# Top-64 attention on one core: threshold counts by ScalarE sums, or by signs summed on TensorE

## The chip, the core and the metric

The kernel runs on one core of a Trainium2 chip. The metric is the device time in microseconds of one execution; smaller is better. The engines are TensorE (PE in the profile, its weight loads PEld), VectorE (DVE), ScalarE (ACT), GpSimd (POOL) and SyncE (SP), which issues the DMAs. Each works through its own list of instructions in order and waits on semaphores for the others.

## What is computed

The reference is one gated cross-attention block with top-k selection and a small quantised feed-forward step, for 32 batches of 256 tokens and width 256:

```python
Q = (layernorm(x) @ Wq.T + bq).reshape(b, 16, 256, 16)      # 16 heads of 256 rows
K, V = ...                                                  # the same from the context
scores = einsum('bhqd,bhkd->bhqk', Q, K) / 4
topk_scores, topk_idx = top_k(scores, 64)                   # 64 of the 256 keys of each row
attn = softmax(topk_scores) @ V[topk_idx]
x = x + tanh(g_xattn) * (attn.reshape(b, 256, 256) @ Wo.T + bo)
x = x + tanh(g_ffn) * fp8_gemm(layernorm(x), kernel) ...    # 256 x 256, then bias
```

The costly part is the selection: 32 batches of 16 heads of 256 rows, each needing its 64 largest of 256 scores. The scores are needed to full precision, so queries and keys are split into three bf16 levels, and a product over 96 rows gives them.

## The kernel before

**Halves and tiles.** A batch has two halves (`g`) of 8 heads; half `i = 2b + g`. A head is two tiles of 128 rows by 256 keys, so a half has 16 tiles (`GT`). `scores` makes the score tiles on PE in `ps_s`, and `copy_scores` on DVE copies them to `score_sb`, with each row's maximum in `mx`. Four halves are held (`RING`).

**Guide rounds.** No row is sorted. A threshold X is looked for of each row, above which some 57 to 64 of its scores lie. It begins at a quarter of the row's maximum (`start_thresholds`). In each of four rounds (`GUIDES`) the scores above it are counted (`guide_counts`): ACT does 15 of the 16 tiles (`ACT_TILES`, L880), each with one Sign of X minus score summed along the row by the accumulator; DVE does the last (L1068). `update_thresholds` (L1072 on) on DVE then steps X, by a slope in round 0 and by a chord between the nearest points on both sides later; a step is a chain of small operations on 128x16, each waiting for the one before it. The next count waits for it (`s_thr`), and it waits for the count (`s_cnt`, `s_dcnt`).

**Final tiles and thresholds.** Once the four rounds of half i are done, and while those of half i + 1 run, `final_tiles` on DVE takes four tiles a round: compare with X and count (L1146), push the scores above X down by a huge number (L1151, four tiles at once), and take the next eight below it (MAX8, L1157). `final_thresholds` picks from these eight, by the count, the 64th score (`thr`) and the 65th. A row where these can't be told apart or found is unsure. PE sums the unsure rows of each tile (`sum_unsure`), DVE reads the sum (`read_unsure`, `convert_unsure`, `settle`) and, where it is not zero, searches the tile in eight rounds of maxima and replacements (`select_tile`, L1192, L1194).

**Masks, exponents, mix.** `masks_of` on ACT (L891) writes `unfit`, Relu of `thr` minus score, which is above zero for a score not selected; it waits for `settle`. `exponents` on PE makes the head's scores again, by key, less the row's maximum, in `ps_e`, and adds the mask times -2^100 (L712, L716). ACT takes the exponential (L900), and `mix` multiplies by the values in f32 (L731). These lag the masks by 2 and 4 heads (`MASK_LAG`, `MIX_LAG`).

**The rest of a batch.** Front: layernorm, transposes, projections q, k, v in f32 (L664 to L686), two or three batches ahead; GpSimd splits q and k in levels, and DMAs lay them out by head. Back: output projection (L742), residual, second layernorm, quantised feed-forward, two or three batches behind. The order of the work is written out by hand in each engine's `batch` function. PSUM's eight banks are `ps_s` (two), `ps_e` (two), `ps_o`, `ps_a`, `ps_b` and `ps_x`.

## Time and profile before

| | |
|---|---|
| median of 3 runs | 3271.35 us (3269.1 to 3274.13) |
| profiled execution | 3268.81 us |
| its span, first to last instruction | 3266.9 us |
| mean granted TensorE clock | 0.717 of full speed |
| busy: PE, DVE, ACT, POOL | 54%, 82%, 84%, 30% |
| DMA | mean 51 GB/s |

A busy share is the time in which the engine had an instruction recorded. Instructions of one engine overlap somewhat in the records, so the cost of one in a row of like ones is read from start to start, not from its duration. A granted clock of 1 is 2.4 GHz, 0.5 is 1.2 GHz; a value between is a mix of the two over the stretch.

### The profile page before, as it was taken

How to read it: one execution, taken by the hardware profiler on the slowest of the kernel's cores; microseconds unless marked ns; L12 is line 12 of the kernel's file. 1: busy time of each engine (PE TensorE's matmuls, PEld its weight loads, DVE VectorE, ACT ScalarE, POOL GpSimd, SP SyncE). 2: the span in 40 equal slices, each digit the busy share in tenths (PEclk: the TensorE clock that was granted, in tenths of full speed). 3: DMA queues.
4: the chain of work that ended last, by engine and by line, in shares of the span. 5: the costliest groups of instructions: out<-in, count | busy, mean ns of one | idle time of the engine just before them, and what ended most of it. 6: DMA issues, size and time to landing. Idle time of an engine off the chain costs nothing.

```text
span 3266.9 us, 51511 instructions
## 1 busy us (share of the span) xinstructions
PE 1780.4 (54%) x7952; PEld 950.5 (29%) x7952; DVE 2691.6 (82%) x11883; ACT 2730.3 (84%) x9638; POOL 966.1 (30%) x1174
## 2 busy tenths in 40 slices
PE   3245555555465555455556556564556556454555
PEld 2122233332233233232323333332233223232222
DVE  1678888888888888888888888888888888888884
ACT  1888888998788898797889998988798788997983
POOL 5122223233222233232233223333223233232112
PEclk8567677777677777776667777767676767777777
DMA  4223332223333223331233333223333133331211
GB/s 70 38 43 60 49 47 52 52 49 63 52 52 54 45 49 63 52 55 34 48 64 56 60 48 56 48 48 64 53 49 55 33 62 61 55 54 33 40 24 46
DMA packets 451902, 166.43 MB, mean 51 GB/s; under 512 B 245616, under 2 KB 451440, under 8 KB 451520
## 3 DMA queue, kind: packets, MB, share of 16 engines
q1 hardware_dynamic: 451136, 162.38, 28.4%
q14 instruction: 310, 2.54, 0.3%
q8 instruction: 72, 1.18, 0.2%
q0 software_dynamic: 384, 0.33, 0.1%
HBM read 102.57 MB, written 59.24 MB: 50 GB/s over the span
## 4 chain that ended last, share of the span: by engine, by line
DVE 36%; ACT 30%; issue 17%; PE 14%; DVEq 2%; POOL 1%; ACTq 0%; DMA 0%; SPq 0%; POOLq 0%; another core or an unknown queue 0%
ACT act_junk L880 22%; DVE masked L1151 5%; DVE score_sb L1047 4%; PE ps_o L731 4%; DVE following L1157 4%; DVE masked L1146 3%; ACT unfit L891 3%; ACT pT_sb L900 2%; PE ps_a L684 2%; DVE X L1083 2%; PE ps_b L675 2%; PE ps_e L712 1%; PE ps_a L686 1%; DVE chord L1115 1%; PE ps_e L716 1%
## 5 line engine op out<-in xcount | busy, mean ns | idle before, releaser
L880 ACT ACTIVATE act_junk<-score_sb,X 128x256 int8<-128x256 f32 x3840 | 1892.1, 503 | 211.3 <-DVE X L1121 183.2
L712 PE MATMUL ps_e<-qs,ks 99*128 99x256 bf16 x1024 | 348.2, 350 | 1321.7 <-ACT pT_sb L900 1321.7
L731 PE MATMUL ps_o<-pT_sb,v_aug 128*32 128x256 f32 x2048 | 766.4, 514 | 0.5 <-ACT pT_sb L900 0.5
L880 ACT ACTIVATION_READ_ACCUMULATOR act_junk<-score_sb,X 128x1 f32 x3840 | 755.0, 197 | 0.0
L891 ACT ACTIVATE unfit<-score_sb,thr 128x256 bf16<-128x256 f32 x1024 | 463.1, 504 | 218.0 <-DVEq L1241 214.6
L1047 DVE TENSOR_SCALAR_CACHE_REDUCE score_sb<-ps_s 128x256 f32<-128x256 f32 x1024 | 418.8, 415 | 142.1 <-PE ps_s L698 140.0
L712 PEld LDWEIGHTS ps_e<-qs,ks 99*128 99x128 bf16 x1024 | 121.9, 119 | 1403.6 <-ACT unfit L891 1199.5
L1146 DVE TENSOR_SCALAR_CACHE_REDUCE masked<-score_sb,X 128x256 f32<-128x256 f32 x1024 | 426.3, 472 | 19.1 <-DVE x_res L1294 8.4
L1157 DVE MAX8 following<-masked 128x8 f32<-128x256 f32 x1024 | 357.7, 409 | 1.7 <-issue 0.7
L540 POOL CAST split<-proj 128x512 bf16<-128x512 f32 x64 | 48.0, 750 | 1042.8 <-ACT proj L866 1027.2
L716 PE MATMUL ps_e<-dropb,unfit 128*128 128x128 bf16 x2048 | 355.9, 273 | 0.0
L1151 DVE SCALAR_TENSOR_TENSOR masked<-masked,score_sb 128x1024 f32<-128x1024 f32 x256 | 336.8, 1316 | 0.4
L900 ACT ACTIVATE pT_sb<-ps_e 128x512 f32<-128x512 f32 x512 | 301.7, 590 | 11.9 <-PE ps_o L731 11.8
L731 PEld LDWEIGHTS ps_o<-pT_sb,v_aug 128*32 128x32 f32 x2048 | 231.9, 136 | 266.4 <-issue 191.0
L716 PEld LDWEIGHTS ps_e<-dropb,unfit 128*128 128x128 bf16 x2048 | 253.3, 124 | 52.4
L698 PE MATMUL ps_s<-ks,qs 96*128 96x256 bf16 x1024 | 228.2, 311 | 67.7 <-DVE score_sb L1047 35.1
L1083 DVE TENSOR_TENSOR X<-aim,count 128x16 f32<-128x16 f32 x256 | 82.3, 322 | 200.8 <-ACT act_junk L880 167.3
L510 POOL TENSOR_SCALAR var<-mv 128x2 f32<-128x2 f32 x64 | 14.6, 228 | 579.4 <-DVE mv L994 576.5
L1068 DVE SCALAR_TENSOR_TENSOR dve_junk<-score_sb,X,minus_twos 128x256 bf16<-128x256 f32 x256 | 158.2, 618 | 0.1
L698 PEld LDWEIGHTS ps_s<-ks,qs 96*128 96x128 bf16 x1024 | 74.8, 102 | 269.8 <-issue 206.2
L602 POOL TENSOR_TENSOR rest<-y_sb,magic_sb 128x512 f32<-128x512 f32 x32 | 43.9, 1371 | 362.4 <-DVE magic_sb L1020 362.4
L559 POOL COPY qs<-rows 96x4096 bf16<-96x4096 bf16 x32 | 127.2, 3974 | 22.7 <-DMA rows<-q_scr 11.6
(158 smaller groups left out, 3332.8 us busy)
## 6 DMA issues: line engine op xcount, KB each, us to landing
rows<-q_scr SPq DMA_DIRECT2D x192, 128.0 KB, 5.1
rows<-k_scr SPq DMA_DIRECT2D x192, 128.0 KB, 5.0
o_scr<-o_sb SPq DMA_DIRECT2D x128, 128.0 KB, 2.7
q_scr<-split SPq DMA_DIRECT2D x32, 384.0 KB, 2.7
k_scr<-split SPq DMA_DIRECT2D x32, 384.0 KB, 2.7
x_in<-in_x SPq DMA_DIRECT2D x32, 256.0 KB, 3.1
ctx_sb<-in_ctx SPq DMA_DIRECT2D x32, 256.0 KB, 2.7
v_scr<-proj SPq DMA_DIRECT2D x32, 256.0 KB, 5.8
```

What stands on the lines that cost most here:

```text
L698: ins = nc.tensor.matmul(ps_s[:, n % 2, jh * TOK:(jh + 1) * TOK], qs[u][0:SPLITS, h, 8 * jh:8 * jh + 8, :].rearrange("d j t -> d (j t)"), ...
L712: nc.tensor.matmul(ps_e[:, n % 2, kc * TOK:(kc + 1) * TOK], ks[u][:, h, 8 * kc:8 * kc + 8, :].rearrange("d j t -> d (j t)"), qs[u][:, h, : ...
L716: ins = nc.tensor.matmul(ps_e[:, n % 2, kc * TOK + jh * P:kc * TOK + jh * P + P], unfit[:, n % MASKS, jh, kc * P:kc * P + P], dropb[:], st ...
L731: ins = nc.tensor.matmul(ps_o[32 * c:32 * c + 32, half * TOK:(half + 1) * TOK], v_aug[p][:, 2 * h + kc, :], pT_sb[:, n % 2, kc * TOK:(kc + ...
L880: ins = nc.scalar.activation(act_junk[:, t, :], score_sb[:, slot, t, :], ACT.Sign, scale=-1.0, bias=X[slot % 2][:, 0, t:t + 1], accum_out= ...
L891: ins = nc.scalar.activation(unfit[:, n % MASKS, jh, :], score_sb[:, slot, t, :], ACT.Relu, scale=-1.0, bias=thr[:, slot, t:t + 1])
L900: nc.scalar.activation(pT_sb[:, n % 2, :], ps_e[:, n % 2, :], ACT.Exp).then_inc(s_PT, 1)
L1047: ins = nc.vector.tensor_scalar(score_sb[:, slot, t, :], ps_s[:, n % 2, jh * TOK:(jh + 1) * TOK], 0.0, None, ALU.add, ALU.max, accum_out=m ...
L1068: ins = nc.vector.scalar_tensor_tensor(dve_junk[:, t - ACT_TILES, :], score_sb[:, slot, t, :], X[slot % 2][:, 0, t:t + 1], minus_twos[:].t ...
L1146: nc.vector.tensor_scalar(masked[:, k, :], score_sb[:, slot, t, :], X[slot % 2][:, 0, t:t + 1], None, ALU.is_gt, ALU.add, accum_out=final_ ...
L1151: nc.vector.scalar_tensor_tensor(masked[:], masked[:], -BIG, scores, ALU.mult, ALU.add).then_inc(s_fin, 1)
L1157: nc.vector.max(following[:, t, 1:], masked[:, k, :]).then_inc(s_fin, 1)
```

## The change

All counts of a guide round go over TensorE. For each of the half's 8 heads PE makes the scores again, this time with the keys on the partitions (`scores_by_key`), in one of three banks `ps_t`. Two more matmuls subtract each row's threshold (`less_thresholds`), from X transposed on PE (`transpose_thresholds`) and negated by ACT into bf16 (`negate_thresholds`). ACT takes one Sign of the head's 128x512 differences from PSUM, with no bias and no accumulator, into bf16 (`signs`). PE sums the signs over the keys with four matmuls by a column of ones (`tally`), and DVE reads the counts from PSUM. So that the subtraction is exact, X is kept as a value that bf16 can hold: each step is written to bf16 first (`started`, `stepped`).

DVE no longer counts a guide tile. The count at the final X, before made by DVE's compare, is now made on ACT, four tiles a round (`final_counts`). DVE's compare and push-down of four tiles becomes one operation a tile, the score times (score not above X). `final_thresholds` has two more small operations. The masks move from ACT to DVE: one compare a tile of the score with `thr`, written as bf16 1 or 0. The exponents share the three banks, and both lags become one of 2 heads. The projections, the output and the feed-forward step share one bank `ps_a`, and the transposed thresholds and counts one, `ps_c`. PE's, ACT's, DVE's and SP's orders are written anew around this.

```diff
@@ PE @@
+            def transpose_thresholds(i, slot, r):
+                pe.wait_ge(s_thr, GUIDES * i + r + 1)
+                pe.wait_ge(s_crd, GUIDES * i + r)
+                nc.tensor.transpose(ps_xt, X[slot][:, 0, :], ident[:]).then_inc(s_xt, 1)
+            def scores_by_key(u, g, n, bank):
+                h = head_of(g, n)
+                for kc in range(2):
+                    nc.tensor.matmul(ps_t[:, bank, kc * TOK:(kc + 1) * TOK],
+                                     ks[u][0:SPLITS, h, 8 * kc:8 * kc + 8, :].rearrange("d j t -> d (j t)"),
+                                     qs[u][0:SPLITS, h, :, :].rearrange("d j t -> d (j t)"), start=(kc == 0), stop=False,
+                                     skip_group_check=True)
+            def less_thresholds(i, r, n, bank):
+                if n == 0:
+                    pe.wait_ge(s_mx, GUIDES * i + r + 1)
+                both_chunks = minus_x[:].rearrange("t (o q) -> t o q", o=1).to_broadcast([GT, 2, P])
+                for jh in range(2):
+                    ins = nc.tensor.matmul(ps_t[:, bank, :].rearrange("p (c j q) -> p c j q", c=2, j=2)[:, :, jh, :],
+                                           identb[0:GT, 2 * n + jh:2 * n + jh + 1].to_broadcast([GT, P]), both_chunks,
+                                           start=False, stop=(jh == 1), skip_group_check=True)
+                ins.then_inc(s_R, 1)
+            def tally(i, par, r, n, buf):
+                pe.wait_ge(s_G, GUIDES * GH * i + GH * r + n + 1)
+                for jh in range(2):
+                    for kc in range(2):
+                        ins = nc.tensor.matmul(ps_cnt[par][:, 2 * n + jh:2 * n + jh + 1],
+                                               sign[:, buf, kc * TOK + jh * P:kc * TOK + jh * P + P], ones_b[:],
+                                               start=(kc == 0), stop=(kc == 1))
+                if n == GH - 1:
+                    ins.then_inc(s_cnt, 1)
+            def count_round(b, p, u, g, r, phase, first, second, last, middle):
...
+                scores_by_key(u, g, 0, bank[0])
+                scores_by_key(u, g, 1, bank[1])
+                less_thresholds(i, r, 0, bank[0])
+                less_thresholds(i, r, 1, bank[1])
+                if last:
+                    exponent_taken(*last)
+                for n in (2, 3):
+                    scores_by_key(u, g, n, bank[n])
+                    less_thresholds(i, r, n, bank[n])
+                    tally(i, slot % 2, r, n - 2, buf[n - 2])
+                if first:
+                    exponents(*first, bank[4], False)
+                if middle:
+                    middle()
+                for n in (4, 5):
+                    tally(i, slot % 2, r, n - 2, buf[n - 2])
+                    scores_by_key(u, g, n, bank[n + 1])
+                    less_thresholds(i, r, n, bank[n + 1])
+                if first:
+                    exponent_taken(*first)
+                for n in (6, 7):
+                    scores_by_key(u, g, n, bank[n + 1])
+                    less_thresholds(i, r, n, bank[n + 1])
+                    tally(i, slot % 2, r, n - 2, buf[n - 2])
+                if second:
+                    exponents(*second, bank[9], False)
+                for n in (6, 7):
+                    tally(i, slot % 2, r, n, buf[n])
@@ PE, batch, each round r @@
+                        if guided:
+                            count_round(cb, cp, cu, cg, r, phase, first, second, last, middle)
...
+                        if has(2) and (g, r) == (0, 0):
+                            transpose_tokens(b + 2)
...
+                        if first:
+                            mix(*first)
+                        if second:
+                            mix(*second)
+                        for k in (2 * r + 2, 2 * r + 3):
+                            if k < GH and has(1):
+                                scores(b + 1, (u + 1) % OPS, g, k, 2 * b + g - 1 if k == 2 and mixes else None)
...
+                        if r < GUIDES - 1 and guided:
+                            transpose_thresholds(2 * cb + cg, 2 * cp + cg, r + 1)
@@ ACT @@
-            def guide_counts(i, slot, r):
...
-            def masks_of(i, slot, n):
...
+            def negate_thresholds(i, r):
+                act.wait_ge(s_xt, GUIDES * i + r + 1)
+                nc.scalar.activation(minus_x[:], ps_xt, ACT.Copy, scale=-1.0).then_inc(s_mx, 1)
+            def signs(i, r, n, buf, bank):
+                act.wait_ge(s_R, GUIDES * GH * i + GH * r + n + 1)
+                nc.scalar.activation(sign[:, buf, :], ps_t[:, bank, :], ACT.Sign).then_inc(s_G, 1)
+            def final_counts(i, slot, t):
...
+                ins = nc.scalar.activation(act_junk[:, t % JUNK, :], score_sb[:, slot, t, :], ACT.Sign, scale=-1.0,
+                                           bias=X[slot][:, 0, t:t + 1], accum_out=final_count[:, t:t + 1])
+            def round_of_signs(i, r, phase, i_final, final_slot, first, second, mixed):
...
+                    negate_thresholds(i, r)
+                for n in range(GH):
+                    if i is not None:
+                        signs(i, r, n, sign_buffer(phase, r, n), bank[n if n < 4 else n + 1])
+                    if n == 3 and first:
+                        exps(*first, bank[4])
+                    if n == 3 and mixed:
+                        evacuate_mixed(*mixed)
+                    if n == 7 and second:
+                        exps(*second, bank[9])
+                    if n % 2 and i_final is not None:
+                        final_counts(i_final, final_slot, 4 * r + n // 2)
@@ DVE @@
-            def guide_counts(i, slot, r):
...
-                nc.vector.tensor_tensor(x[:, 1, :], aim[:], count[slot % 2][:], ALU.subtract).then_inc(s_upd, 1)
+                nc.vector.tensor_scalar(x[:, 1, :], ps_cnt[slot % 2], TOK - 2 * AIM, None, ALU.add).then_inc(s_crd, 1)
...
-                nc.vector.tensor_tensor(newton[:], newton[:], x[:, 0, :], ALU.add)
+                nc.vector.tensor_tensor(stepped[:, 0, :], newton[:], x[:, 0, :], ALU.add)
...
-                    nc.vector.tensor_scalar(masked[:, k, :], score_sb[:, slot, t, :], X[slot % 2][:, 0, t:t + 1], None,
-                                            ALU.is_gt, ALU.add, accum_out=final_count[:, t:t + 1]).then_inc(s_fin, 1)
+                    nc.vector.scalar_tensor_tensor(masked[:, k, :], score_sb[:, slot, t, :], X[slot][:, 0, t:t + 1],
+                                                   score_sb[:, slot, t, :], ALU.is_le, ALU.mult).then_inc(s_fin, 1)
...
-                nc.vector.scalar_tensor_tensor(masked[:], masked[:], -BIG, scores,
-                                               ALU.mult, ALU.add).then_inc(s_fin, 1)
...
+            def masks_of(i, slot, n):
+                H = GH * i + n
+                dve.wait_ge(s_T, at(H - MASKS + 1))
+                carry(dve)
+                for jh in range(2):
+                    t = 2 * n + jh
+                    ins = nc.vector.tensor_scalar(unfit[:, n % MASKS, jh, :], score_sb[:, slot, t, :], thr[:, slot, t:t + 1], None,
+                                                  ALU.is_lt)
+                ins.then_inc(s_P, 1)
@@ SP, batch @@
+                if has(1):
+                    store_values(b + 1)
                 if has(3):
                     load_front(b + 3)
...
+                if has(-1):
+                    move_out(b - 1)
                 if has(1):
                     move_values(b + 1, 1 - p)
-                if has(-1):
-                    move_out(b - 1)
```

On DVE a round r of half i is now: four products of the final tiles, two copies of scores, the read of the unsure rows (round 0), four maxima, two copies, `settle` (round 0), four masks, `start_thresholds` (round 3), the update of half i + 1's thresholds, in round 3 mixed with `final_thresholds` of half i, and then the pieces of the front and the back.

## Rows read from the trace of the kernel before

**Rows 1.** The page: busy time, share and instructions of each engine.
```profile
PE 1780.4 (54%) x7952; PEld 950.5 (29%) x7952; DVE 2691.6 (82%) x11883; ACT 2730.3 (84%) x9638; POOL 966.1 (30%) x1174
```

**Rows 2.** One line by itself, L880: ns min/median/max, first and last start.
```profile
L880 ACT ACTIVATE act_junk<-score_sb,X x3840: 491/501/542, 81.0 to 3174.8; 128x256 int8<-128x256 f32 x192
```

**Rows 3.** Timeline of ACT, two stretches: start us, duration us, instruction, count.
```profile
1608.33 0.49 ACT L880 ACTIVATE act_junk<-score_sb,X 128x256 int8<-128x256 f32 x1
...
1608.82 0.49 ACT L880 ACTIVATE act_junk<-score_sb,X 128x256 int8<-128x256 f32 x1
...
1691.27 0.35 ACT L907 COPY o_sb<-ps_o 128x256 f32<-128x256 f32 x1
1691.52 0.59 ACT L900 ACTIVATE pT_sb<-ps_e 128x512 f32<-128x512 f32 x1
1692.01 0.90 ACT L891 ACTIVATE unfit<-score_sb,thr 128x256 bf16<-128x256 f32 x2
```

**Rows 4.** Groups by line: busy us, mean ns, idle before and its releasers.
```profile
L880 ACT ACTIVATE act_junk<-score_sb,X 128x256 int8<-128x256 f32 x3840 | 1892.1, 503 | 211.3 <-DVE X L1121 183.2 <-DVE X L1058 23.3 <-DVE X L1101 4.5
```

**Rows 5.** Windows: stretch, busy us of each engine, granted clock, DMA share, GB/s.
```profile
1618.00:1620.00 2.00, 2.00 (x5) 0.69 (x6) 1.78 (x10) 2.00 (x7) 0.00 (x0) 0.50 0.00 0
1626.00:1628.00 2.00, 0.00 (x0) 0.00 (x0) 1.29 (x12) 2.00 (x7) 0.00 (x0) 0.76 0.00 0
3190.00:3204.00 14.00, 12.21 (x74) 6.59 (x72) 12.94 (x43) 7.12 (x16) 3.52 (x6) 0.99 0.18 42
```

**Rows 6.** Timeline of PE where the granted clock is at its upper level.
```profile
3197.03 0.27 PE L712 MATMUL ps_e<-qs,ks 99*128 99x256 bf16 x1 [1.05 <-ACT pT_sb L900]
...
3197.25 0.27 PE L712 MATMUL ps_e<-qs,ks 99*128 99x256 bf16 x1
...
3197.56 1.05 PE L731 MATMUL ps_o<-pT_sb,v_aug 128*32 128x256 f32 x4
3198.55 0.28 PE L712 MATMUL ps_e<-qs,ks 99*128 99x256 bf16 x1
...
1604.84 0.66 PE L664 MATMUL ps_a<-ident,xn_sb 128*128 128x128 f32 x4
...
1605.77 0.38 PE L698 MATMUL ps_s<-ks,qs 96*128 96x256 bf16 x2
...
1309.76 0.81 PE L675 MATMUL ps_a<-xT,wT 128*128 128x256 f32 x3
1310.41 0.38 PE L698 MATMUL ps_s<-ks,qs 96*128 96x256 bf16 x2
```

**Rows 7.** Timeline of DVE: first and last step of one threshold update, one copy between.
```profile
1604.83 0.15 DVE L1083 TENSOR_TENSOR X<-aim,count 128x16 f32<-128x16 f32 x1
...
1605.93 0.41 DVE L1047 TENSOR_SCALAR_CACHE_REDUCE score_sb<-ps_s 128x256 f32<-128x256 f32 x1
...
1606.27 0.17 DVE L1101 COPY_PREDICATED X<-far,newton 128x16 f32<-128x16 int32 x1
...
1607.61 0.18 DVE L1121 COPY_PREDICATED X<-both,chord 128x16 f32<-128x16 int32 x1
```

**Rows 8.** DVE groups by line, and then its tile of a count by itself.
```profile
L1146 DVE TENSOR_SCALAR_CACHE_REDUCE masked<-score_sb,X 128x256 f32<-128x256 f32 x1024 | 426.3, 472 | 19.1 <-DVE x_res L1294 8.4 <-issue 2.3 <-DVE following L1157 0.2
...
L1151 DVE SCALAR_TENSOR_TENSOR masked<-masked,score_sb 128x1024 f32<-128x1024 f32 x256 | 336.8, 1316 | 0.4
...
L1068 DVE SCALAR_TENSOR_TENSOR dve_junk<-score_sb,X,minus_twos 128x256 bf16<-128x256 f32 x256 | 158.2, 618 | 0.1
...
L1068 DVE SCALAR_TENSOR_TENSOR dve_junk<-score_sb,X,minus_twos x256: 474/480/2452, 87.1 to 3169.2; 128x256 bf16<-128x256 f32 x128
```

**Rows 9.** The searches: their maxima by line, and two in the timeline of DVE.
```profile
L1192 DVE MAX8 max<-masked x56: 427/428/429, 403.2 to 2960.5; 128x8 f32<-128x256 f32 x56
...
403.22 0.43 DVE L1192 MAX8 max<-masked 128x8 f32<-128x256 f32 x1
...
404.20 0.43 DVE L1192 MAX8 max<-masked 128x8 f32<-128x256 f32 x1
```

More of the change, by code:

```diff
@@ L56 @@
 QUARTER = GT // GUIDES
-MASK_LAG, MIX_LAG = 2, 4
+MIX_LAG = 2
+BANKS = 3
+SIGNS = 3
+JUNK = 4
 def at(count):
@@ L120, in build @@
         AB = sb("AB", [P, 2, GT])
-        count = [sb(f"count{k}", [P, GT]) for k in range(2)]
-        aim = sb("aim", [P, GT])
+        sign = sb("sign", [P, SIGNS, 2 * TOK], BF16)
+        minus_x = sb("minus_x", [GT, P], BF16)
         newton = sb("newton", [P, GT])
@@ new lines, in batch @@
+                        mixed = None
+                        if r == 3 and mixes:
+                            mixed = mb, mg, 0
+                        if r == 1 and mixes and has(-1):
+                            mixed = (b - 1, g, 1)
+                        round_of_signs(2 * b + g + 1 if guided else None, r, phase, 2 * b + g, 2 * p + g,
+                                       lagged(2 * r), lagged(2 * r + 1), mixed)
+                        if has(2) and (g, r) == (0, 0):
+                            evacuate_tokens(b + 2)
@@ L1348, in batch @@
                         ending = final_thresholds(i, slot) if last else iter(())
-                        next(steps, None)
-                        for jh in range(2):
-                            next(ending, None)
-                            next(steps, None)
-                        for jh in range(2):
-                            next(ending, None)
-                            if has(1) and not last:
-                                copy_scores(i + 2, fresh, 2 * r + 1, jh)
-                            next(steps, None)
                         for _ in ending:
```

475 lines of the change are left out of this document (259 added, 216 removed).

## The prediction

> **What bounds the kernel now.** I read the page first. VectorE (DVE) is busy 82% of the span, ScalarE (ACT) 84%, TensorE (PE) 54% [rows 1]; two full engines and one half idle. The unit to think in is one guide round: one count of all 16 tiles of a half and the threshold step that follows. There are 32 x 2 = 64 halves of four, so 256 rounds; the count line's first and last instructions give their extent, 81.0 to 3174.8 plus one of 0.5, 3094.3 us, or **12.09 us a round**, and 172.6 us outside them [rows 2]. The timeline of ACT shows what a round costs there: counts start every 0.49 us, the read of the accumulator beneath the next [rows 3], so 15 make 7.4 us; four masks, two exponentials and a share of evacuations at the same pitch make some 3.3 us more. That is 10.7 of 12.09. The line view names a part of the rest: ACT sat idle 211 us in all before a count, most of it until DVE's last step on X [rows 4]. So ACT and DVE hand the round to and fro, and both are nearly full. PE is not in it, and pays for its pauses: in the windows it works a whole 2 us at granted clock 0.50 (1.2 GHz) after a pause, has lost the upper level again after an idle stretch, and holds 0.99 (2.4 GHz) where it is busy 12.2 of 14 us [rows 5].
>
> **The change, per round, at the upper clock.** Pitches on PE from starts in a stretch at that clock [rows 6]: one 256-column bf16 matmul and two of 128 columns, each with its weight load, take 0.22, so 256 columns are 0.11; exponents of a head 0.53 with the switch, of which 0.44 is streaming; mix of a head 0.99; three 256-column f32 records 0.65, so 0.22 each; transposes of both inputs 0.93.
>
> *Added on PE:* 16 matmuls of scores by key and 16 that subtract the threshold, 256 columns each: 32 x 0.11 = 3.5. Then 32 tallies, each a load of 128 columns and one column of work. No such pair is in the trace. Three loads with their matmuls fit in 0.22, so a load takes at most 0.07; below, two loads and 128-column matmuls in 0.11 give 0.055; from above, I bound the pair by the 0.11 of a 256-column matmul. I take 0.07, 0.28 a head, 2.2 a round, because the load has nothing to hide behind but is no longer than 0.07. The transpose of X, some 0.3, makes 6.0 us added.
>
> *Kept on PE:* two heads of exponents (0.88), of mix (1.98) and scores (0.44), and once in each of the eight rounds of a batch one extra: 0.49, 0.44, 1.73, 0.23, 1.73, 0.44, 1.73, 2.6 (transposes of tokens and context, q, quantised transposes, k, feed-forward matmul, output, values; 8, 8 and 12 f32 records by 0.22), mean 1.17.
>
> *Removed on ACT:* 15 counts and 4 masks. *Added:* 8 Signs of 128x512 without an accumulator; the nearest row is the exponential of the same shape, start to start 0.49 [rows 3]; four final counts at 0.49; a negation of 16x128. ACT comes to 8 x 0.49 + 4 x 0.49 + 2 x 0.49 + 0.3 + 0.6 = 7.8 us, from 10.7: no longer a bound.
>
> **The round walked.** Time 0 is the first subtraction. Signs 0 to 7 wait in turn for PE; ACT between Sign 0 and the end of Sign 7 also has three final counts and one exponential: 12 x 0.49 = 5.9, and starts at 0.42 (two subtractions and a handover), so Sign 7 ends at 6.6 and its tally at 7.05. PE's own work in that stretch is 6 x 0.22 + 8 x 0.22 + 8 x 0.28 + 2 x 0.44 = 6.2, so it fits with 0.85 to spare; three banks keep it two heads ahead. A copy of mixed values (0.25, [rows 3]) in half of the rounds adds 0.12. Then two things run beside each other. DVE steps the thresholds: the chain takes 1604.83 to 1607.79, less two copies of scores of 0.34 between [rows 7], so 2.3, and 2.5 with handovers (1.3 in round 0, none in front of the next half's round 0, whose threshold is there already). PE does the extra, two mixes and two scores: 2.42 plus the extra, 2.91, 2.86, 4.15, 2.65, 4.15, 2.86, 4.15, 5.02, mean 3.59, more than the step in every round. So the steps of the thresholds are hidden behind PE, and PE's list is what is late next. Last, transpose, negation and handovers 0.85, with the next two scores by key beneath. Sum: 7.05 + 0.12 + 3.59 + 0.85 = **11.61 us a round**.
>
> **DVE.** It is busy 2691.6/256 = 10.5 a round. Gone: the 1024-column mask step (1.32) and its own tile of the count (0.62). The accumulating compare (0.47) becomes a product with two inputs; nearest row its own guide tile's median 0.48, so nothing is counted either way [rows 8]. Added: four masks without accumulator, at most that 0.48 each and, at half of it, 0.24; I take 0.3, 1.2 a round, because the result is half as wide and nothing is summed. Small ones: 0.1. DVE 9.9 a round, 8.2 to 10.6, against 11.61: hidden, if it is not held up. It is less than PE's sum only by 1.7; with that cover gone each further 0.1 costs 26 us. Masks are due one round before their exponents, and copies one round before the scores behind them, so neither is a wait. In round 0 of a half DVE reads the sum of unsure rows that PE makes only after four heads: behind it queue the maxima, two copies, the masks, all needed by the next step; I count some 4 us from there to the end of the counting, just enough.
>
> **Slow searches.** A tile whose boundary is not found is searched in 8 rounds, 0.98 each, with the lead some 9 us; 56 maxima are 7 searches [rows 9]. Guiding values kept as bf16 move the count by less than one row, against a window of eight, so I keep 7, at 63 us, fully exposed (before they are inside the 12.09).
>
> **SP's queue.** The store of the values goes ahead of the load of the next inputs, and the move of the mixed values ahead of the values' spread. DMAs are as many as before, and what counting waits for is DVE, not a DMA [rows 4]; I count nothing.
>
> **Sum.** 256 x 11.61 = 2972, outside 173, searches 63: 3208 span; with 1.9 us around the span and 2.5 us from the profiled run to the median, **3213 us**, 1.8% less than 3271.35.
>
> **Two rules weighed.** In the rows above a load of 128 columns takes at most 0.07 when others lie around it. The Trainium skill (TensorE: Matmul & The Clock Gate, LDWEIGHTS) gives columns over 1.2 GHz, an estimate of 107 ns: tallies 0.43 a head, 1.2 us more a round, of which PE's spare time in the sign phase takes some 0.35, about 3430 us; three loads in 0.22 us speak against it here. The accumulating compare of 128x256 has mean 472, while its two-input guide tile has median 480, mean 618 and maximum 2452 [rows 8]: something blocks the latter at times. The Trainium skill (SBUF — State Buffer, Who interferes with whom) says that VectorE and GpSimd take one port pair in turn for operations with two SBUF inputs and for plain tensor_scalar, not for the accumulating form; it speaks against this change, which turns four immune operations a round into exposed ones and adds four.
>
> **Rivals.**
> *DVE held up (slower).* Exposed operations per round go from 2 to 8. At the excess of that tile, 0.138 each [rows 8], that is 0.8 us more, DVE 10.7, and with round 0's read (up to 2.5, 0.6 on average) 11.3: no cover is left and lateness reaches PE. ACT before waited 0.82 a round for DVE [rows 4]; the same here gives 3213 + 211 = 3424, half of it 3319. It decides from 0.22 a round. For: the maximum. Against: DVE has 1.7 spare and much less is due inside a step. The port rule above would land here.
> *PE's clock falls (slower).* PE waits for Signs in bursts. At mean clock c its 10.6 us become 10.6/c; 0.98 eats the gain, 0.9 gives 12.8 a round, 3515. For: [rows 5] before, pauses do this. Against: 85% busy held 0.99, and here it is 91%. The Trainium skill (same TensorE page, A second HAM failure mode) describes matmul groups cycling through PSUM banks whose short idles keep dropping the clock; no run here shows such a pattern.
> *The faster end.* If tallies take 0.055 and PE, not ACT, were to set less of the sign phase, the step binds: 7.17 + 2.6 + 0.85 = 10.6 where there is no extra, 11.1 on average: 3085.
> *The steering gets worse.* If bf16 values leave twice as many boundaries unfound, 63 us more: 3276, no change; the tally's unsure rows would show it.
>
> **How the numbers follow.** PE-paced as summed 0.40, its own range 3150 to 3265; faster end 0.16 (3085); DVE held up 0.25 (3320 to 3424, a part of it only 3270 to 3300); clock 0.12 (over 3300); worse steering 0.07. I give 3213; low 3075, high 3420, which leaves out the deep end of the clock case and half of the fast end. A measurement tells 0.2% (6.5 us) from no change. Faster: 0.40 + 0.16 = 0.56; same 0.06, from worse steering and the mild end of held-up DVE; slower 0.38.
>
> **What would show it.** PE busy about 90% at granted clock 0.95 or more; Sign at 0.49 start to start; eight Signs in 6 to 6.5 us; tally pairs of 0.06 to 0.08; ACT some 65% busy; DVE near 85%; waits of ACT for PE, and of PE little for anything; 56 maxima in searches. I am wrong if PE's transposes wait for DVE's X (DVE paces), if granted clock stays near 0.7, or if tallies take over 0.1.

## Result: 15% slower, because TensorE fell to its lower clock

The changed kernel takes 3755.66 us (median, 3746.12 to 3778.08) against 3270.22 for the kernel before on the same chip: ratio 1.1494 [1.1441, 1.1547]. The prediction was 3213, with 3075 to 3420. One of its rivals, "PE's clock falls", names what happened, but it was given 0.12. Clocks given beside a time here and below are those of the profiled execution.

The page of the changed kernel, busy time of each engine and TensorE's granted clock in 40 slices, against [rows 1]:

```profile
PE 3525.1 (94%) x24592; PEld 1780.6 (47%) x24592; DVE 2502.6 (67%) x11235; ACT 2129.1 (57%) x5286; POOL 919.7 (25%) x1172
...
PE   4799999999989999999999999999999899998994
...
PEclk8556766676766666766666666667666666666657
```

TensorE is now the full engine, at 94%, VectorE and ScalarE have a third or more to spare, and yet the clock row stands at 5 to 7 tenths nearly throughout (mean 0.666). The prediction had PE at about 90% with 0.95 or more. The negation that opens each round, by itself (ns min/median/max, first and last start):

```profile
L1022 ACT ACTIVATE minus_x<-ps_c x256: 267/267/268, 108.1 to 3641.4; 16x128 bf16<-16x128 f32 x128
```

From 108.1 to 3641.4 are 255 rounds: 13.86 us a round, where 11.61 was predicted and [rows 2] had 12.09. In the groups by line (busy us, mean ns, idle before and its releaser) ScalarE's idle time ahead of it ends with PE's transpose, so PE sets the pace:

```profile
L1022 ACT ACTIVATE minus_x<-ps_c 16x128 bf16<-16x128 f32 x256 | 68.4, 267 | 640.9 <-PE ps_c L739 640.9
```

The windows of the changed kernel (us, busy time of each engine, granted clock, DMA share, GB/s) show why the round is long; [rows 5] are the same view of before:

```profile
1600.00:1610.00 10.00, 10.00 (x73) 4.60 (x72) 5.44 (x28) 6.24 (x15) 0.00 (x0) 0.50 0.00 1
1612.00:1618.00 6.00, 5.98 (x63) 2.99 (x63) 5.93 (x19) 5.53 (x15) 4.28 (x9) 1.00 0.11 32
...
1626.00:1634.00 8.00, 8.00 (x56) 4.24 (x55) 3.44 (x21) 5.57 (x14) 0.00 (x0) 0.50 0.03 4
1636.00:1642.00 6.00, 6.00 (x60) 3.08 (x58) 5.86 (x20) 4.73 (x13) 4.30 (x5) 1.00 0.00 0
```

In both kinds of window PE is busy all the time by the records. In the first it is granted 0.50 (1.2 GHz) for 10 us and makes 73 matmuls, in the second 1.00 (2.4 GHz) and makes 63 in 6 us. Before, a low clock stood beside a pause; in these windows no pause is recorded. What a head costs at either level is in PE's timeline (start, duration, instruction, count; the duration of a record is modelled, so read the starts). First a stretch at 0.50, then one at 1.00, then the mixes of two heads at 1.00:

```profile
1601.84 0.59 PE L745 MATMUL ps_t<-qs,ks 96*128 96x256 bf16 x2
1602.36 0.60 PE L756 MATMUL ps_t<-minus_x,identb 16*128 16x256 bf16 x2
1602.89 0.26 PE L766 MATMUL ps_c<-ones_b,sign 128*128 128x1 bf16 x4
1603.02 0.59 PE L745 MATMUL ps_t<-qs,ks 96*128 96x256 bf16 x2
...
1613.34 0.38 PE L745 MATMUL ps_t<-qs,ks 96*128 96x256 bf16 x2
1613.65 0.39 PE L756 MATMUL ps_t<-minus_x,identb 16*128 16x256 bf16 x2
1613.97 0.25 PE L766 MATMUL ps_c<-ones_b,sign 128*128 128x1 bf16 x4
1614.09 0.27 PE L782 MATMUL ps_t<-qs,ks 99*128 99x256 bf16 x1
...
1635.86 1.06 PE L840 MATMUL ps_o<-pT_sb,v_aug 128*32 128x256 f32 x8
1636.86 0.61 PE L730 MATMUL ps_s<-ks,qs 96*128 96x256 bf16 x4
```

L745 is the scores by key, L756 the subtraction over 16 rows, L766 the tally, L840 the mix. A head takes 0.52 + 0.53 + 0.13 = 1.18 us at the lower level and 0.31 + 0.32 + 0.12 = 0.75 at the upper one. Three things were not foreseen. Two 256-column matmuls were to take 0.22 by [rows 6], and take 0.31; at the lower level they take 0.52 where the columns alone would make some 0.43. So about 0.1 us is lost each time PE goes from one of the two kinds to the other. And four tallies, loads included, take 0.12 at either level, not 0.28. The third is the mix: its eight matmuls for two heads, now in a row, take 1.00 together, where in [rows 6] the four of one head took 0.99. (At the lower level two heads take 1.86.)

The groups of the changed kernel that answer to the other steps:

```profile
L1027 ACT ACTIVATE sign<-ps_t 128x512 bf16<-128x512 f32 x2048 | 1162.9, 606 | 390.2 <-PE ps_t L756 387.7
...
L756 PEld LDWEIGHTS ps_t<-minus_x,identb 16*128 16x128 bf16 x4096 | 261.7, 99 | 542.7 <-issue 460.0
...
L1240 DVE TENSOR_SCALAR X<-ps_c 128x16 f32<-128x16 f32 x256 | 44.6, 174 | 516.5 <-PE ps_c L766 512.9
```

And two lines by themselves, the masks and the write-back after a search:

```profile
L1371 DVE TENSOR_SCALAR unfit<-score_sb,thr x1024: 334/346/2983, 214.6 to 3700.1; 128x256 bf16<-128x256 f32 x171
...
L1359 DVE TENSOR_SCALAR score_sb<-masked x5: 381/382/3561, 498.8 to 3396.4; 128x256 f32 x5
```

Signs wait for PE (387.7 us), VectorE's first step of a round waits for PE's tallies (512.9 us), and the load of the 16-row matmuls is late with nothing that it waited for by the profile (460.0 us). The masks take 0.35 at the median with a tail to 2.98.

### The profile page after: what moved, and what is told of

The parts are those of the page before. It is cut to its first block and busy times, and to the rows that moved or that the text cites. A ratio compares the mean times of both kernels' runs of the same rounds, so it can differ in the third digit from the quotient of the medians.

```text
span 3751.2 us, 83563 instructions
## 1 busy us (share of the span) xinstructions
PE 3525.1 (94%) x24592; PEld 1780.6 (47%) x24592; DVE 2502.6 (67%) x11235; ACT 2129.1 (57%) x5286; POOL 919.7 (25%) x1172
## 5 line engine op out<-in xcount | busy, mean ns | idle before, releaser
L1027 ACT ACTIVATE sign<-ps_t 128x512 bf16<-128x512 f32 x2048 | 1162.9, 606 | 390.2 <-PE ps_t L756 387.7
L756 PE MATMUL ps_t<-minus_x,identb 16*128 16x256 bf16 x4096 | 936.9, 327 | 0.0
L745 PE MATMUL ps_t<-qs,ks 96*128 96x256 bf16 x4096 | 929.8, 329 | 0.0
L766 PEld LDWEIGHTS ps_c<-ones_b,sign 128*128 128x128 bf16 x8192 | 377.5, 105 | 419.5 <-ACT sign L1027 240.6
L1035 ACT ACTIVATE act_junk<-score_sb,X 128x256 int8<-128x256 f32 x1024 | 530.4, 518 | 8.3 <-DVE following L1299 8.2
L756 PEld LDWEIGHTS ps_t<-minus_x,identb 16*128 16x128 bf16 x4096 | 261.7, 99 | 542.7 <-issue 460.0
L766 PE MATMUL ps_c<-ones_b,sign 128*128 128x1 bf16 x8192 | 502.0, 169 | 7.4 <-ACT sign L1027 6.3
L840 PE MATMUL ps_o<-pT_sb,v_aug 128*32 128x256 f32 x2048 | 440.5, 553 | 6.9 <-ACT pT_sb L1045 6.9
L1302 DVE SCALAR_TENSOR_TENSOR masked<-score_sb,X 128x256 f32<-128x256 f32 x1024 | 428.1, 479 | 16.3 <-DVE x_res L1470 7.5
L1371 DVE TENSOR_SCALAR unfit<-score_sb,thr 128x256 bf16<-128x256 f32 x1024 | 391.8, 443 | 63.1 <-issue 53.1
L745 PEld LDWEIGHTS ps_t<-qs,ks 96*128 96x128 bf16 x4096 | 313.0, 105 | 185.1 <-issue 147.6
L1240 DVE TENSOR_SCALAR X<-ps_c 128x16 f32<-128x16 f32 x256 | 44.6, 174 | 516.5 <-PE ps_c L766 512.9
L786 PE MATMUL ps_t<-dropb,unfit 128*128 128x128 bf16 x2048 | 356.2, 273 | 0.0
L782 PE MATMUL ps_t<-qs,ks 99*128 99x256 bf16 x1024 | 341.5, 344 | 6.0 <-ACT pT_sb L1045 4.2
L840 PEld LDWEIGHTS ps_o<-pT_sb,v_aug 128*32 128x32 f32 x2048 | 149.4, 145 | 208.9 <-issue 175.6
L730 PE MATMUL ps_s<-ks,qs 96*128 96x256 bf16 x1024 | 214.9, 348 | 28.6 <-POOL ks L579 19.8
```

What stands on the lines that cost most here:

```text
L745: nc.tensor.matmul(ps_t[:, bank, kc * TOK:(kc + 1) * TOK], ks[u][0:SPLITS, h, 8 * kc:8 * kc + 8, :].rearrange("d j t -> d (j t)"), qs[u][0 ...
L756: ins = nc.tensor.matmul(ps_t[:, bank, :].rearrange("p (c j q) -> p c j q", c=2, j=2)[:, :, jh, :], identb[0:GT, 2 * n + jh:2 * n + jh + 1 ...
L766: ins = nc.tensor.matmul(ps_cnt[par][:, 2 * n + jh:2 * n + jh + 1], sign[:, buf, kc * TOK + jh * P:kc * TOK + jh * P + P], ones_b[:], star ...
L782: nc.tensor.matmul(ps_t[:, bank, kc * TOK:(kc + 1) * TOK], ks[u][:, h, 8 * kc:8 * kc + 8, :].rearrange("d j t -> d (j t)"), qs[u][:, h, :, ...
L786: ins = nc.tensor.matmul(ps_t[:, bank, kc * TOK + jh * P:kc * TOK + jh * P + P], unfit[:, n % MASKS, jh, kc * P:kc * P + P], dropb[:], sta ...
L840: ins = nc.tensor.matmul(ps_o[32 * c:32 * c + 32, half * TOK:(half + 1) * TOK], v_aug[p][:, 2 * h + kc, :], pT_sb[:, n % 2, kc * TOK:(kc + ...
```

## The experiments

Three theories of the slowdown, and the prediction's second rival. **A, rows:** matmuls over 16 rows keep PE busy but don't hold its clock at the upper level. **B, switch:** the 0.1 us at each change between few-row and wide matmuls is what costs, and the clock is another matter. **C, pauses:** PE's short waits for Signs drop the clock. **DVE held up:** VectorE, with eight more operations that something can block, is late. Ratios are against the kernel before, timed beside each kernel.

**Subtraction over 96 and over 128 rows.** The negated thresholds lie in a taller tile whose other rows are zero, and the selecting columns come from as many rows of the identity. What is computed, TensorE's columns and its instructions stay as they are; only the rows that take part change. With 96 rows:

```
-        minus_x = sb("minus_x", [GT, P], BF16)
+        minus_x = sb("minus_x", [96, P], BF16)
...
+            nc.gpsimd.memset(minus_x[:], 0.0).then_inc(s_id, 1)
...
-                both_chunks = minus_x[:].rearrange("t (o q) -> t o q", o=1).to_broadcast([GT, 2, P])
+                both_chunks = minus_x[:].rearrange("t (o q) -> t o q", o=1).to_broadcast([96, 2, P])
...
-                                           identb[0:GT, 2 * n + jh:2 * n + jh + 1].to_broadcast([GT, P]), both_chunks,
+                                           identb[0:96, 2 * n + jh:2 * n + jh + 1].to_broadcast([96, P]), both_chunks,
...
-                nc.scalar.activation(minus_x[:], ps_xt, ACT.Copy, scale=-1.0).then_inc(s_mx, 1)
+                nc.scalar.activation(minus_x[0:GT], ps_xt, ACT.Copy, scale=-1.0).then_inc(s_mx, 1)
```

> The changed kernel with the subtraction of the thresholds made over 96 rows, 80 of them zeros, in place of 16; same columns, same results. In the changed kernel a pair of 256-column matmuls next to a 16-row pair takes 0.32 us at the upper clock and 0.53 at the lower, 0.1 more than its columns, and the granted clock falls in stretches in which PE never pauses. Theory A (rows: work over 16 rows does not hold the clock up, and PE at a low clock sets the time): the mean granted clock rises from 0.67 to 0.9 or more, rounds of 11.6 to 12 us, 3150 to 3300 us. Theory B (switch: each change between 16-row and wide matmuls costs 0.1 us, the clock is another matter): the clock stays near 0.67, two switches a head by 8 heads by 256 rounds by 0.1 are 410 us less, about 3350 us. Theory C (pauses of PE for ACT and DVE lower the clock): both stay, about 3750 us.

Measured: 3398.13 us, ratio 1.0368 [1.0347, 1.039], clock 0.833. PE's timeline of this kernel, first at the upper level, then at the lower:

```profile
1603.55 0.38 PE L746 MATMUL ps_t<-qs,ks 96*128 96x256 bf16 x2
1603.76 0.38 PE L757 MATMUL ps_t<-minus_x,identb 96*128 96x256 bf16 x2
1603.98 0.24 PE L767 MATMUL ps_c<-ones_b,sign 128*128 128x1 bf16 x4
...
1609.13 0.64 PE L746 MATMUL ps_t<-qs,ks 96*128 96x256 bf16 x2
1609.56 0.63 PE L757 MATMUL ps_t<-minus_x,identb 96*128 96x256 bf16 x2
1609.98 0.29 PE L767 MATMUL ps_c<-ones_b,sign 128*128 128x1 bf16 x4
```

Two matmuls take 0.21 and 0.22, or 0.43 and 0.42, as their columns say: the loss at the change is gone, and the tallies over 128 rows that follow bring none. Neither theory had this right in size. A wanted a clock of 0.9 or more and 3150 to 3300 us; B wanted 3350 us, which is nearer to what was measured, but with the clock left near 0.67. The clock rose by 0.167 and the loss went, so this run alone can't weigh them against each other.

> As the run with 96 rows, but 128 rows, 112 of them zeros. Theory A: the clock is at least that of 96 rows, 0.9 or more. Theory B: if any change of the number of rows costs a switch, the pairs still take 0.32 and 0.53 us and the time stays near 3750; if only the change to 16 rows does, as with 96 rows, about 3350 us with the clock near 0.67. Theory C: about 3750 us.

Measured: 3297.74 us, ratio 1.0069 [1.0052, 1.0086], clock 0.887. PE's share is down to 78%, with the same instructions:

```profile
PE 2586.6 (78%) x24592; PEld 1787.4 (54%) x24592; DVE 2640.2 (80%) x11343; ACT 2065.2 (63%) x5286; POOL 921.4 (28%) x1173
...
PEclk8789888999989899888999999998989888888985
```

The clock is just under the 0.9 that A asked for. 458 us come back by adding rows of zeros. New waits show behind them; these are the longest of PE in the list of waits of the 128-row kernel (us in total, times, longest):

```profile
PE ps_c L767 <- ACT sign L1028: 186.4, 674, 1.5
PE ps_c L740 <- DVE X L1280: 162.1, 74, 4.1
PE ps_s L882 <- DVE score_sb L1214: 126.6, 59, 3.2
```

L882 is the sum of unsure rows, which PE makes in the middle of a half's first round. It waits 2.1 us for VectorE's copy of scores in 59 of 64 halves. PE's timeline shows one such wait, and VectorE's shows the copies queued behind the four products for the maxima:

```profile
1611.29 0.20 PE L882 MATMUL ps_s<-unsure_b,ones_c 128*1 128x16 f32 x2 [2.38 <-DVE score_sb L1214]
...
1608.88 1.66 DVE L1303 SCALAR_TENSOR_TENSOR masked<-score_sb,X 128x256 f32<-128x256 f32 x4
1610.46 0.42 DVE L1214 TENSOR_SCALAR_CACHE_REDUCE score_sb<-ps_s 128x256 f32<-128x256 f32 x1
```

**A filler on PE.** The 16-row kernel, with one matmul of 128 rows and 256 columns more per head; the scores by key overwrite its result.

```
+                nc.tensor.matmul(ps_t[:, bank, 0:TOK], dropb[:], kq_sb[:, 0, :], start=True, stop=True, skip_group_check=True)
                 for kc in range(2):
                     nc.tensor.matmul(ps_t[:, bank, kc * TOK:(kc + 1) * TOK],
```

> The changed kernel with one more bf16 matmul of 128 rows by 256 columns in front of each head's scores by key, whose result is overwritten; PE has 2048 matmuls more, results unchanged. Theory A (too little work over many rows in the counting stretch): the mean granted clock rises above 0.8, and the time falls in spite of the added 0.11 to 0.21 us a head, to 3450 to 3650 us. Theory B and C: the clock stays near 0.67, and 8 x 256 x 0.16 us come on top, about 4080 us.

Measured: 3672.06 us, ratio 1.1223 [1.1204, 1.1241], clock 0.811. Three lines of its timeline of PE:

```profile
1613.97 0.27 PE L744 MATMUL ps_t<-kq_sb,dropb 128*128 128x256 bf16 x1
1614.08 0.38 PE L746 MATMUL ps_t<-qs,ks 96*128 96x256 bf16 x2
1614.39 0.39 PE L757 MATMUL ps_t<-minus_x,identb 16*128 16x256 bf16 x2
```

The full engine was given 2048 x 0.11 = 225 us of useless work, kept its losses at the changes (0.31), and the kernel became 84 us faster (3755.66 to 3672.06). Of what the traces show, only the clock can pay for that: 0.666 to 0.811 (0.805 at the median of its executions). The time missed A's 3450 to 3650 us by a little; B and C, at about 4080 us with the clock unmoved, missed by much more.

**The kernel before, its masks on VectorE.** The `Relu` masks leave ScalarE; the compares are put where the changed kernel has them.

```
-                    ins = nc.scalar.activation(unfit[:, n % MASKS, jh, :], score_sb[:, slot, t, :], ACT.Relu, scale=-1.0,
-                                               bias=thr[:, slot, t:t + 1])
+                    ins = nc.vector.tensor_scalar(unfit[:, n % MASKS, jh, :], score_sb[:, slot, t, :], thr[:, slot, t:t + 1], None,
+                                                  ALU.is_lt)
```

> The kernel before, with one part of the change alone: the masks of the exponents made by DVE as bf16 compares, four a round behind the search, in place of ACT's four Relus. If the transfer of load decides (DVE 10.5 us busy of 12.09 a round, plus 4 x 0.28 to 0.35, ACT less 1.6): DVE is the bound, 3350 to 3500 us, ACT's idle time grows. If the waits decide (ACT sat idle 218 us in all before its masks, for the search), these go away and the time falls to 3100 to 3200 us.

Measured: 3480.89 us, ratio 1.0632 [1.0614, 1.065]. The counts' line of this kernel:

```profile
L880 ACT ACTIVATE act_junk<-score_sb,X 128x256 int8<-128x256 f32 x3840 | 1892.2, 498 | 1021.6 <-DVE X L1108 456.8 <-DVE X L1088 435.0 <-DVE X L1045 129.7
```

Against [rows 4], ScalarE's wait for VectorE grew from 211.3 to 1021.6 us. With VectorE nearly full (88% busy), this part of the change alone costs 6%, inside the 3350 to 3500 us expected if the transfer of load decides.

**Subtraction over 64 rows.** The same edit with 64 in place of 96.

> As the runs with 96 and 128 rows, the subtraction over 64 rows, 48 of them zeros. With 96 and 128 rows a pair next to another takes 0.22 us at the upper clock and 0.43 at the lower, with 16 rows 0.32 and 0.53; the clock was 0.67, 0.83, 0.89 and the time 3755, 3398, 3298 us. Theory A (rows) wants the mean clock between those of 16 and 96 rows, about 0.76. If the switch cost belongs to few rows (two of four groups of 32 included), pairs stay at 0.32 and 0.53 and the time is 3520 to 3650 us; if it belongs to one group of 32 alone, it is gone, and the time is 3430 to 3500 us. Against theory A: a clock as with 96 rows.

Measured: 3525.71 us, ratio 1.0784 [1.0759, 1.0809], clock 0.807. Its timeline of PE at the upper level:

```profile
1600.73 0.38 PE L746 MATMUL ps_t<-qs,ks 96*128 96x256 bf16 x2
1601.04 0.39 PE L757 MATMUL ps_t<-minus_x,identb 64*128 64x256 bf16 x2
1601.37 0.25 PE L767 MATMUL ps_c<-ones_b,sign 128*128 128x1 bf16 x4
```

The starts are 0.31 and 0.33 apart, as with 16 rows, so the loss at the changes is whole. The spacings at either level are those of 16 rows (0.31 and 0.32, 0.52 and 0.54 at the median), so from 16 to 64 rows the clock is what moved, and it was worth 230 us. This is the run that parts A from B. It didn't land where A was put in numbers, though: A wanted some 0.76, and 0.807 is near the 0.833 of 96 rows. From 64 to 96 rows the loss goes and the clock rises by 0.026: 128 us for both together. From 96 to 128: clock 0.054 up, 100 us.

**The 16-row kernel, its masks back on ScalarE.** The compares leave VectorE's queue, and `Relu` masks stand at the end of ScalarE's round.

```
-                        if mixes:
-                            masks_of(i - 1, mixed, 2 * r)
-                            masks_of(i - 1, mixed, 2 * r + 1)
...
+                        if mixes:
+                            masks_of(2 * mb + mg, 2 * mp + mg, 2 * r)
+                            masks_of(2 * mb + mg, 2 * mp + mg, 2 * r + 1)
```

> The changed kernel (16 rows) with the masks back on ACT, as four Relus at the end of each round of signs, where ACT waits 641 us in all for PE. If PE at a low clock sets the time (theory A), this is worth little: within 1% of 3755 us, the clock stays near 0.67. If DVE, held up by masks and by GpSimd on the port pair, sets it, the time falls by 4 x 0.28 us and more a round, to below 3470 us.

Measured: 3762.47 us, ratio 1.149 [1.1471, 1.1509], clock 0.66. As A expected, relieving VectorE of 1024 operations does nothing: it was not what held the kernel back.

**128 rows, and VectorE's copies ahead of its products.** In a half's first round the two copies of scores go before the products.

```
-                        next(finals)
+                        if r:
+                            next(finals)
                         if has(1):
                             copy_scores(i + 2, fresh, 2 * r, 0)
                             copy_scores(i + 2, fresh, 2 * r, 1)
+                        if not r:
+                            next(finals)
```

> The subtraction over 128 rows, and in round 0 of a half DVE makes its two copies of scores in front of the four products, not behind them. With 128 rows PE stood 127 us in all in front of the sum of unsure rows, for such a copy, some 2.4 us in each of 59 halves, in the middle of its counting. If that stall is on the path, it goes and the time falls by 60 to 130 us from 3298, to about 3200 us, with the clock up a little; if DVE sets the round anyway, it stays within 0.5% of 3298.

Measured: 3263.56 us, ratio 0.9968 [0.9955, 0.998]; 34 us less than with 128 rows alone. PE's wait for the sum of unsure rows fell from 126.6 to 43.3 us. The gain lies between the two cases expected (60 to 130 us, or within 0.5%): the stall was on the path only in part.

**The same, with the masks on ScalarE too** (the two edits above together).

> The same with the masks back on ACT as well (four Relus behind the last count of a round). DVE had 2640 us of work with 128 rows, of which the masks are 396; PE waited 258 us for its steps of X. If DVE is what is late once the clock is up, this falls by another 100 to 250 us, to 2950 to 3100 us, below both kernels; if PE's own work sets it, about 3200 us; if the Relus stand in the way of the next round's signs, above 3250 us.

Measured: 3167.54 us (3162.06 to 3173.57), ratio 0.9683 [0.9665, 0.9701], clock 0.915. The page of this kernel, then the negation by itself:

```profile
PE 2543.1 (80%) x24592; PEld 1738.4 (55%) x24592; DVE 2259.5 (71%) x10319; ACT 2433.0 (77%) x6310; POOL 920.6 (29%) x1173
...
PEclk8689899999989999999889999998999899998987
```

```profile
L1023 ACT ACTIVATE minus_x<-ps_c x256: 250/267/268, 109.3 to 3052.9; 16x128 bf16<-16x128 f32 x128
```

(3052.9 - 109.3) / 255 = 11.54 us a round, and the wait of the sum of unsure rows fell from 126.6 to 19.8 us, in the list of PE's waits:

```profile
PE ps_s L882 <- DVE score_sb L1230: 19.8, 28, 2.0
```

This version beats both kernels, by 3.2% and 15.7%. The same move of the masks that did nothing with 16 rows gives 96 us here, where PE's slowness no longer hides VectorE. That is just short of the 100 to 250 us expected if VectorE is what is late; at 3167.54 the time is as near to the 3200 us expected if PE's own work sets it, so the run does not single out one bound.

**Scores of two heads in a row, 16 rows.** For heads 2 and 3, 4 and 5, and 6 and 7, both scores by key come before both subtractions; a tally still stands between the two scores. The edit for heads 2 and 3:

```
-                for n in (2, 3):
-                    scores_by_key(u, g, n, bank[n])
-                    less_thresholds(i, r, n, bank[n])
-                    tally(i, slot % 2, r, n - 2, buf[n - 2])
+                scores_by_key(u, g, 2, bank[2])
+                tally(i, slot % 2, r, 0, buf[0])
+                scores_by_key(u, g, 3, bank[3])
+                less_thresholds(i, r, 2, bank[2])
+                less_thresholds(i, r, 3, bank[3])
+                tally(i, slot % 2, r, 1, buf[1])
```

> The changed kernel with its 16-row subtractions, in another order: the scores by key of two heads back to back, then the subtractions of the two, so that TensorE changes between few-row and wide matmuls half as often. Theory B (about 0.1 us is lost at each change between them) expects some 8 changes fewer a round, up to 0.8 us a round, 3550 to 3700 in all. Theory A alone (the clock goes by the share of work over few rows, and the order is nothing) expects the time of the changed kernel within 2%, 3680 to 3790, and a clock near 0.67 in both.

Measured: 3759.89 us, ratio 1.1493 [1.1465, 1.1521], clock 0.663, so no effect. PE's timeline of it, at the upper level:

```profile
1617.83 0.39 PE L745 MATMUL ps_t<-qs,ks 96*128 96x256 bf16 x2
1618.37 0.25 PE L766 MATMUL ps_c<-ones_b,sign 128*128 128x1 bf16 x4
1618.48 0.38 PE L745 MATMUL ps_t<-qs,ks 96*128 96x256 bf16 x2
1618.79 0.61 PE L756 MATMUL ps_t<-minus_x,identb 16*128 16x256 bf16 x4
1619.33 0.25 PE L766 MATMUL ps_c<-ones_b,sign 128*128 128x1 bf16 x4
1619.45 0.27 PE L782 MATMUL ps_t<-qs,ks 99*128 99x256 bf16 x1
```

Four matmuls of 16 rows take 0.54, where twice two take 0.64, so the saving is there. But the tally that now stands between the two scores comes 0.54 us after them, not 0.22 or 0.31; by the profile its load waited for the Sign. The pair takes 1617.83 to 1619.45, 1.62 us, against 2 x 0.75 = 1.50 in the changed kernel. The order gives its saving back at once, so this run agrees with A and tells little of B's price.

**The best version with the filler, and with the paired order.** Both edits as above, on the 3167.54 us version.

> The 128-row subtractions with VectorE's two copies first and the masks on ScalarE (3167.5 us at a clock of 0.915), with one extra 128-row matmul of 256 columns a head, whose result is overwritten. If what is left in a round is TensorE's clock, the clock rises to 0.95 or more and the time stays or falls, 3120 to 3180. If it is the chain of ScalarE's signs and VectorE's products, the 0.11 us added a head lies on the path at least in part and the time rises, 3200 to 3320.

Measured: 3181.97 us, ratio 0.9711 [0.9685, 0.9738], clock 0.938; the interval [0.9685, 0.9738] overlaps with the [0.9665, 0.9701] of the version without filler.

> The 128-row subtractions with VectorE's two copies first and the masks on ScalarE, with the scores by key of two heads back to back before their subtractions. The loss at each change between few-row and wide matmuls was gone with 96 and 128 rows, so theory B expects nothing of it: within 1% of 3167.5. If the changes still cost something with 128 rows, it is 1 to 3% faster. A later first sign of each pair would show as up to 2% slower.

Measured: 3198.2 us, ratio 0.9773 [0.9744, 0.9802], clock 0.913.

A filler of 225 us at the upper level moves the time by 14 us, within the intervals. A likely reading, not shown, is that it lies mostly in time in which PE waits, and that the little clock that it brings pays for some of the rest. Neither the clock nor PE's sum is the single bound now: the expected 3200 to 3320 of a chain with the filler on it did not come, nor a gain, nor the clock of 0.95. The pairing costs 1%, within the up to 2% expected from a later first Sign where there is no change to save; that the Sign is the reason is not shown.

## Why the prediction was wrong

**The step that failed** is "Against: 85% busy held 0.99, and here it is 91%". It took the clock to follow PE's busy share. (The share in that window is 12.21 of 14 us, 87%; the slip changes nothing.) The window at 3190 in [rows 5] from which this came held exponents over 99 rows and mixes over 128, no matmul over 16; here half of the 32 matmuls of 256 columns that a round gains are over 16. At 94% busy the clock was 0.666. With the same instructions over 64, 96 and 128 rows it was 0.807, 0.833 and 0.887, while the busy share fell to 78%. The filler shows it from the other side, with no row changed in the subtractions. Theory A stands on both, and on the run with 64 rows above all, in which the loss at the changes stayed.

**Pauses.** C, the pauses, falls as the cause of the low clock here: in the window at 1600 PE is busy 10.00 of 10 us at 0.50, and with 128 rows PE waits for Signs more (186.4 us against 6.3) at a higher clock. The traces can be counted through as well (without the start and the end of the kernel), for the idle time of PE in the 5 us ahead of each fall from the upper level to the lower. With 16 rows, 173 of 207 falls had less than 0.3 us of it; with 64 rows 43 of 120; with 96 and 128 rows, and in the kernel before, none of 104, 104 and 212. That is not for want of such stretches: with 96 rows 39% of all stretches of 5 us had so little. So pauses do stand ahead of every fall where the matmuls are wide, and what is new with 16 rows is falls without one. The Trainium skill (TensorE: Matmul & The Clock Gate, A second HAM failure mode), named by the prediction for this rival, describes short idles between groups; most falls of the changed kernel came without any. Of rows the Trainium skill (TensorE: Matmul & The Clock Gate, Step-by-step) says that their count doesn't matter for the time of a weight load. The load records agree (median 95 ns over 16 and 64 rows, 98 over 96 and 128), but the rows moved the clock.

**The rival's price.** It put PE's 10.6 us at 10.6/c and stopped at c = 0.9. At 0.666 its formula would make a round of 16.9 us, and 13.86 was measured. Two things in it were off. The first is the shape: a head goes from 0.75 to 1.18 us, a factor of 1.57 and not 2, since tallies and losses at the changes cost the same at both levels. The second is the sum of PE's work. From the median spacings of everything that PE does, I estimate 9.3 us a round at the upper level and 16.2 at the lower, a factor of 1.74. The clock within the rounds was 0.66, which is 68% of the time at the lower level, so work moves at 0.68/1.74 + 0.32 = 0.71 of its upper pace; 9.3/0.71 = 13.1, and with the 0.4 us of recorded pauses 13.5, against 13.86.

**PE's terms.** Mixes: predicted 1.98 for two heads, measured 1.00, the largest miss of the sum. Every round makes two of them in a row here, and the prediction priced each as one that stands alone; the traces show the time, not why. Transpose of X: 0.3 predicted, 0.11 measured. Tallies: predicted 0.28 a head, measured 0.12 at either level. The Trainium skill's estimate of 107 ns a load (TensorE: Matmul & The Clock Gate, LDWEIGHTS) would make 0.43, and no run here shows that in the spacing; records of single loads do last 105 ns on average, but they overlap. The change between the two kinds of matmul: predicted nothing, measured 0.2 a head. Together 0.72 predicted against 0.75, two errors that cancel. Without the loss, with 96 and 128 rows, the head takes 0.21 + 0.22 + 0.11 = 0.54. So PE had 1.3 us a round less to do than predicted, and the clock more than ate it.

**Sign phase.** Eight Signs were to set 7.05 us of a round. In the round at 1612 us, at a granted clock of 0.96, it took 6.90 us from the first subtraction to the end of the last tally, so the size was right at that clock. In the next round, at 0.59, it took 8.91 with PE busy all the time. Over the whole kernel Signs wait 387.7 us for PE. Where PE is at the upper level most of the time the round is 11.54, near the 11.61 that the walk gave, but with the masks on ScalarE, two copies moved, the mixes half their price and a clock of 0.915. That agreement is in good part luck.

**VectorE.** 9.9 us a round predicted; 2502.6/256 = 9.8 measured. Masks: 0.3 predicted, 0.35 median and 0.44 mean measured, with the tail to 2.98 that the rival feared. The rival "DVE held up" did not decide here, as the 16-row kernel with masks on ScalarE shows, but only since PE was later still. With 128 rows VectorE's load does tell: 96 us for the masks, 34 us for the copies behind the products. How much of that is blocked time, the rival's own mechanism, and how much is plain work, no run parts; and that the total (3297.74) lies close to the rival's milder figure of 3319 is luck, since the clock was 0.887. The step "I count some 4 us from there to the end of the counting, just enough" asked only when VectorE reads the sum. It left out that PE, to make the sum in the middle of the counting, first needs VectorE's copy of scores, and PE waits 2.1 us for it in 59 of 64 halves once it is fast enough.

**Searches.** Seven were kept and five came, by the write-back's count. That says nothing of bf16 thresholds, for the count is not the same in every run: all eleven experiments have eight, the kernel before with masks moved (f32 thresholds) as well as the ten with bf16 thresholds. With eight in both kinds, no run shows that bf16 values steer worse. SP's queue was counted at nothing, and nothing in PE's or VectorE's waits points to it.

**What stays open.** Whether the clock follows the rows alone or the rows in company with columns and order; why the mixes of two heads in a row take the time of one; what share of the 128 us between 64 and 96 rows is the loss at the changes; and why that loss is there with 16 and 64 rows and not between 96 and 128. The profile calls the late loads "issue", which names no cause.

## What to carry to other kernels

A TensorE that is busy is not a TensorE at its upper clock. Before work moves to it, ask what rows its matmuls use, take the clock only from stretches with the same kinds of matmul, and price the plan at both levels. Take the price of an operation from rows where it stands as it will stand in the new order: two mixes in a row cost half of what two alone cost. If a matmul has few rows, padding them with zeros costs no instruction and here won 12%. And when one engine is slow, the others' lateness is hidden: price the next bound with it gone, since moving the masks gave nothing in one version and 3% in the other.

## What was not expected of the hardware

- Rows of zeros raise TensorE's clock: the same 24592 matmuls with 16, 64, 96 and 128 rows in 4096 of them ran at a mean granted clock of 0.666, 0.807, 0.833 and 0.887.
- 2048 useless matmuls over 128 rows made a kernel with a 94% busy TensorE 84 us faster, at a clock of 0.811 in place of 0.666.
- About 0.1 us is lost between matmuls over 96 rows and matmuls over 16 or 64, in both directions and at both clock levels (0.31 for 0.22 us, 0.52 for 0.43), and none between 96 and 128.
- Four loads of 128 columns with a one-column matmul each take 0.12 us together at either level.
- Eight f32 matmuls for the mixes of two heads, each head in its own 32 columns, take 1.00 us at the upper level; the four of one head by themselves take 0.99.
